# Channel attention and a look-up-table FFN: Wo loaded early, x groups issued from ScalarE, look-up results built in the low parts' place

## The reference

```python
x = x + attn(layernorm(x), Wq, Wk, Wv, Wo)
x = x + ffn(layernorm(x), lut, gate_idx, up_idx, down_idx)

def attn(x, Wq, Wk, Wv, Wo):           # attention over channels, not over tokens
    qT, kT, vT = (swapaxes(x @ w, 1, 2) for w in (Wq, Wk, Wv))
    weights = softmax(einsum('bes,bfs->bef', qT, kT) / 4)      # 512 x 512 a batch
    return swapaxes(einsum('bef,bfs->bes', weights, vT), 1, 2) @ Wo

def ffn(x, lut, gate_idx, up_idx, down_idx):
    gate, up = x @ lut[gate_idx].T, x @ lut[up_idx].T
    return (silu(gate) * up) @ lut[down_idx].T
```

## Time and profile before

| | |
|---|---|
| median of 3 runs | 1040.51 us (1039.37 to 1041.04) |
| the profiled execution | 1041.32 us; its span 1039.2 us, mean granted clock 0.993 |
| TensorE busy | 1000.8 us, 96% of the span |
| VectorE, ScalarE, GpSimd busy | 485.5, 449.5, 140.4 us |
| VectorE busy from 240 to 360 us | 118.69 of 120 us |

### The profile page before, as it was taken

How to read it: one execution, slowest core, us unless ns; L and a number is a source line. 1 busy time by engine, 2 the same in 40 slices (tenths; PEclk the granted TensorE clock), 3 DMA queues, 4 the chain that set the end, 5 groups by cost and what they waited for, 6 DMA issues and landing times.

```text
span 1039.2 us, 12623 instructions
## 1 busy us (share of the span) xinstructions
PE 1000.8 (96%) x4612; PEld 825.3 (79%) x4612; DVE 485.5 (47%) x1019; ACT 449.5 (43%) x720; POOL 140.4 (14%) x149
## 2 busy tenths in 40 slices
PE   5999889999989999999999999999999999999998
PEld 4988768787777778888888888888888888888886
DVE  5899899899999942312131213111311131112001
ACT  4898798879998821121222122212221222122111
POOL 2332300000000000111111011101110111011111
PEclk9999989999999999999999999999999999999999
DMA  8899902300112182200220002002200020001001
GB/s 258 201 162 147 175 20 86 130 21 34 51 49 72 63 307 98 82 1 1 81 81 1 1 1 82 1 1 81 81 1 1 1 81 1 1 1 41 1 1 40
DMA packets 45050, 65.89 MB, mean 63 GB/s; under 512 B 22128, under 2 KB 32256, under 8 KB 40448
## 3 DMA queue, kind: packets, MB, share of 16 engines
q1 hardware_dynamic: 31808, 56.70, 16.5%
q0 software_dynamic: 8864, 6.43, 5.5%
q10 hardware_dynamic: 4320, 1.97, 0.7%
HBM read 44.05 MB, written 25.10 MB: 67 GB/s over the span
## 4 chain that ended last, share of the span: by engine, by line
PE 83%; DVE 9%; issue 3%; ACT 2%; POOL 1%; DMA 1%; POOLq 0%; SPq 0%; ACTq 0%; DVEq 0%
PE bank L1014 41%; PE bank L1022 21%; PE bank L956 14%; PE bank L1038 4%; DVE part L1181 2%; DVE bn L1158 1%; PE bank L970 1%; PE bank L1003 1%; DVE picked L1181 1%; POOL rstd L726 1%; ACT part L764 1%; DMA xg<-in_L_attn_x 1%; DVE xg_lo L1200 1%; DVE part L1225 1%; DVE bit_mask L1188 0%
## 5 line engine op out<-in xcount | busy, mean ns | idle before, releaser
L1014 PE MATMUL bank<-x2t_hi,w_hi 128*128 128x512 f32 (+1 forms) x704 | 276.3, 392 | 10.8 <-DVE w_lo L1200 7.1
L1014 PE MATMUL bank<-x2t_lo,w_hi 128*128 128x512 f32 (+1 forms) x704 | 275.3, 391 | 0.0
L1014 PE MATMUL bank<-x2t_hi,w_lo 128*128 128x512 f32 (+1 forms) x704 | 275.2, 391 | 0.0
L1405 DVE TENSOR_TENSOR h_full<-bank,h_gate 128x512 f32<-128x512 f32 (+1 forms) x66 | 45.6, 691 | 396.0 <-PE bank L1014 396.0
L1014 PEld LDWEIGHTS bank<-x2t_hi,w_hi 128*128 128x128 f32 (+1 forms) x704 | 130.9, 186 | 42.7 <-DVE w_lo L1200 9.0
L764 ACT ACTIVATE part<-high_bit,lut,lut_step 128x512 f32<-128x512 uint8 x198 | 154.0, 811 | 16.1 <-DVE part L1181 11.0
L1014 PEld LDWEIGHTS bank<-x2t_lo,w_hi 128*128 128x128 f32 (+1 forms) x704 | 131.2, 186 | 29.8
L1014 PEld LDWEIGHTS bank<-x2t_hi,w_lo 128*128 128x128 f32 (+1 forms) x704 | 131.2, 186 | 29.2
L721 POOL TENSOR_TENSOR h_lo<-h_full,h_hi 128x512 fp32r<-128x512 f32 (+1 forms) x66 | 85.3, 1292 | 507.4 <-ACT h_hi L932 507.4
L929 ACT ACTIVATE h_gate<-bank 128x512 f32<-128x512 f32 (+1 forms) x66 | 39.5, 598 | 256.4 <-PE bank L1014 256.4
L1022 PE MATMUL bank<-w_hi,h_hi 128*128 128x512 f32 (+1 forms) x324 | 129.8, 401 | 0.1
(11 more groups left out here) (145 smaller groups left out, 1291.9 us busy)
## 6 DMA issues: line engine op xcount, KB each, us to landing
xg<-in_L_attn_x SPq DMA_DIRECT2D x7, 1024.0 KB, 6.4
x1a<-in_L_attn_x SPq DMA_DIRECT2D x4, 1024.0 KB, 4.8
out_dram<-x1a SPq DMA_DIRECT2D x4, 1024.0 KB, 4.2
x1b<-in_L_attn_x SPq DMA_DIRECT2D x3, 1024.0 KB, 4.9
m_hi<-m_scratch SPq DMA_DIRECT2D x3, 1024.0 KB, 4.8
m_lo<-m_scratch SPq DMA_DIRECT2D x3, 1024.0 KB, 8.2
out_dram<-x1b SPq DMA_DIRECT2D x3, 1024.0 KB, 3.9
h_scratch<-h_kept_hi SPq DMA_DIRECT2D x10, 256.0 KB, 2.0
```

The lines of the kernel that those rows point to most:

```text
L1014: last = pe.matmul(tile[0:n, :], a, x, start=(k == 0 and j == 0), stop=(k == K - 1 and j == 2))
L1405: dve.tensor_tensor(h_full[0:n, :], bank[5][0:n, :], h_gate[0:n, :], ALU.mult).then_inc(h_done, 1)
```

## The change

1. **Wo** gets four tiles `raw_o` of its own (where `x1a` will lie later), which SP loads one after the other after the last piece of Wq. The load of the first x block into `x1` waits for the last split of Wo.
2. **x groups** 3 to 7 are issued by ScalarE: group 3 after the second normalised tile, group g + 3 after the first normalised tile of group g.
3. **Index transfers** stand at other items; the turns of units 0 to 2 are at 6 to 8 rather than 9 to 11, and early stores go to an item that is a multiple of 4.
4. **Head of the Gram stage**: two statistics of group 1 before `gram_low` 1, two after; `gram_low` 2 ahead of `stats_shift` 2. Where a group begins, `gram_in` stands before `gram_n`.
5. **The look-up's result** is built where `w_lo` of the unit will lie; `low` then works in place. The two `picked` tiles are gone, the other leaves have seven tiles: those for j = 2 and 3 are doubled, so that they wait for merges of unit u - 2 and not u - 1. The waits for space that stood ahead of `w_hi` in five units (12, 15, 21, 27, 30) stand ahead of leaf 0.
6. **New tables** `ACT_LOOKS` and `DVE_LOOKS`.

The diff, cut to its core (tile addresses, helpers' signatures and most of the tables are left out):

```diff
@@
         all_tiles = at("all_tiles", 0, [P, 101, D], F32)
...
+        W_PLACE, Y_PLACE, PART_PLACE, Z_PLACE = 94, 95, 97, 99
+        def place_of(u, j):
+            one, five = PART_PLACE + u % 2, PART_PLACE + 1 - u % 2
+            y, z = Y_PLACE + u % 2, Z_PLACE + u % 2
+            return {0: (w_at[u // 3] + 6) // 2 + u % 3, 1: one, 2: y, 3: z, 4: W_PLACE, 5: five, 6: one, 7: z}[j]
...
-            if u and j in (1, 2, 3, 5):
-                eng.wait_ge(merged, merge_count(u - 1, {1: M_45, 2: M_RY, 3: M_67, 5: M_WX}[j]))
+            if u and j in (1, 5):
+                eng.wait_ge(merged, merge_count(u - 1, {1: M_45, 5: M_WX}[j]))
+            if u >= 2 and j in (2, 3):
+                eng.wait_ge(merged, merge_count(u - 2, {2: M_RY, 3: M_67}[j]))
...
-            if j == 0 and u >= 2:
-                eng.wait_ge(w_lo_done, u - 1)
+            if j == 0 and u == 12:
+                eng.wait_ge(product_done, K * (number[(MIX, 0)] + 1))
...
-        narrow_at = [2, 10, 16, 24, 30, 34]
-        turn_at = [9, 10, 11, 16, 18, 20, 22, 24, 26, 28, 29, 30] + list(range(31, 52))
-        store_at = [place + 2 for place in turn_at]
+        narrow_at = [2, 10, 18, 28, 32, 36]
+        turn_at = [6, 7, 8, 14, 15, 16, 22, 24, 26, 27, 28, 29, 32, 33, 34, 35, 36, 37] + list(range(38, 53))
+        store_at = [-(-(place + 2) // 4) * 4 if place < 28 else place + 2 for place in turn_at]
...
+            if i == 0:
+                timeline += [("stats_of", (1, t)) for t in range(2)]
             if i + 1 < T * NG:
                 timeline.append(("gram_low", i + 1))
             if i == 0:
-                timeline += [("stats_of", (1, t)) for t in range(T)]
+                timeline += [("stats_of", (1, t)) for t in range(2, T)]
                 settle(2)
+            if i == 1:
                 timeline.append(("stats_shift", 2))
...
-                if g >= 4:
-                    sp.wait_ge(xg_normed, T * (g - 3))
-                sp.dma_start(xg[g % 4][:], xb_dram[g]).then_inc(xg_loaded[g % 4], 16)
...
                     if arg == (WQ, K - 1):
+                        for k in range(K):
+                            sp.dma_start(raw_o[k][:], wo_in[k * P:(k + 1) * P, :]).then_inc(raw_o_loaded[k], 16)
                         sp.wait_ge(xg_normed, T * 7)
...
-                act.copy(w_hi[c][:, kind, :], picked[u % 2][:]).then_inc(w_hi_done, 1)
+                act.copy(w_hi[c][:, kind, :], tile_of(u, 0)).then_inc(w_hi_done, 1)
...
+                    if i == 1:
+                        load_gram(3)
+                    if t == 0 and 1 <= g and g + 3 < NG:
+                        load_gram(g + 3)
...
                 if stage == "raw":
                     w, k = arg
                     r = K * w + k
-                    act.wait_ge(raw_loaded[r % 2], 16 * (r // 2 + 1))
                     if w == WO:
+                        act.wait_ge(raw_o_loaded[k], 16)
                         act.wait_ge(product_done, K * (number[(PROD, 1)] + 1))
...
-                low(w_lo[c][:, kind, :], picked[u % 2][:], w_hi[c][:, kind, :]).then_inc(w_lo_done, 1)
+                low(w_lo[c][:, kind, :], tile_of(u, 0), w_hi[c][:, kind, :]).then_inc(w_lo_done, 1)
```

More of the change, by code:

```diff
@@ L99, in preln_attention_ghost_ffn @@
         raw_v = [at(f"raw_v{k}", 156 + 2 * k, [P, D], F32) for k in range(K)]
+        raw_o = [at(f"raw_o{k}", 48 + 2 * k, [P, D], F32) for k in range(K)]
         raw = [at(f"raw{i}", 184 + 2 * i, [P, D], F32) for i in range(2)]
@@ L171, in preln_attention_ghost_ffn @@
         raw_loaded = [sem(f"raw_loaded{i}") for i in range(2)]
+        raw_o_loaded = [sem(f"raw_o_loaded{k}") for k in range(K)]
         raw_v_loaded = [sem(f"raw_v_loaded{k}") for k in range(K)]
@@ L287, in make_leaf @@
                 eng.wait_ge(merged, merge_count(u, {6: M_01, 7: M_23}[j]))
-            if j == 0 and u >= 2:
-                eng.wait_ge(w_lo_done, u - 1)
-            return tile_of(u, j)[:], high_bit[u % 2][:], lut_step[:, j:j + 1], lut[:, j:j + 1]
+            if j == 0 and u == 12:
+                eng.wait_ge(product_done, K * (number[(MIX, 0)] + 1))
+            if j == 0 and u == 15:
+                eng.wait_ge(product_done, K * (number[(FOLD, 0)] + 1))
+            if j == 0 and u == 21:
+                eng.wait_ge(m_stored, 16 * 2 * B)
+            if j == 0 and u == 27:
+                eng.wait_ge(x2_turned, 2 * K)
+            if j == 0 and u == 30:
+                eng.wait_ge(second_stored, 16)
+            return tile_of(u, j), high_bit[u % 2][:], lut_step[:, j:j + 1], lut[:, j:j + 1]
         timeline = []
@@ L335, in preln_attention_ghost_ffn @@
                     settle(g + 2)
-            if i + AHEAD + 1 < T * NG:
-                timeline.append(("gram_n", i + AHEAD + 1))
-            if i + AHEAD < T * NG:
-                timeline.append(("gram_in", i + AHEAD))
+            steps = [(name, i + ahead) for name, ahead in (("gram_n", AHEAD + 1), ("gram_in", AHEAD)) if i + ahead < T * NG]
+            timeline += steps if (i + AHEAD + 1) % T else steps[::-1]
             index_steps(i)
@@ L594, in _ @@
                     turn_idx(arg)
-                if stage == "gram" and arg % T == 2 and 4 <= arg // T + 4 < NG:
-                    load_gram(arg // T + 4)
                 if stage == "raw":
                     after = K * arg[0] + arg[1] + 1
-                    if after < K * WV:
+                    if after < K * WO:
                         load_raw(after // K, after % K)
                     if arg == (WQ, K - 1):
+                        for k in range(K):
+                            sp.dma_start(raw_o[k][:], wo_in[k * P:(k + 1) * P, :]).then_inc(raw_o_loaded[k], 16)
                         sp.wait_ge(xg_normed, T * 7)
@@ L757, in fetch_idx, with load_gram @@
                 act.dma_start(idx_in[u % 3][:], idx_dram[u]).then_inc(idx_back[u % 3], 16)
+            def load_gram(g):
+                if g >= 4:
+                    act.wait_ge(xg_normed, T * (g - 3))
+                act.dma_start(xg[g % 4][:], xb_dram[g]).then_inc(xg_loaded[g % 4], 16)
             def make_leaves(u, some):
@@ L1177, in stats_shift, with merge @@
                                          op1=ALU.mult).then_inc(done, 1)
-            def merge(bit, keep, other):
-                return dve.copy_predicated(keep[:], bit_mask[bit][:], other[:])
+            def merge(u, bit, keep, other):
+                return dve.copy_predicated(tile_of(u, keep), bit_mask[bit][:], tile_of(u, other))
             def pairs_of(byte):
@@ L1215, in look_up @@
                 for u in range(U):
[L1216 removed]
                     dve.wait_ge(bits_found, 3 * u + 1)
                     dve.wait_ge(leaf_made, leaf_count(u, 0))
[L1219 removed]
+                    merge(u, 0, 0, 1).then_inc(merged, 1)
                     yield
                     dve.wait_ge(leaf_made, leaf_count(u, 2))
[L1222 removed]
+                    merge(u, 0, 2, 3).then_inc(merged, 1)
                     yield
@@ L1243, in look_up @@
                     dve.wait_ge(leaf_made, leaf_count(u, 7))
-                    merge(0, one, z).then_inc(merged, 1)
+                    merge(u, 0, 6, 7).then_inc(merged, 1)
                     yield
```

67 lines of the change are left out of this document (29 added, 38 removed).

## The result

The changed kernel takes 1036.45 us (median of 9 runs, 1034.69 to 1037.34) against 1040.65 (9 runs) for the one before; the ratio is 0.9954, interval 0.9943 to 0.9965, so 3.6 to 5.9 us less. It is faster, but by about half of the 9.5 us forecast (4.8 by the ratio, 4.2 by the medians): inside the whole range, above the likeliest case's own 1028 to 1034. The profiled execution took 1034.96 with a span of 1032.9, 6.3 less than the span before. It is one of the faster ones.

The account below looks back on a forecast made before the run. VectorE's idle time until unit 31's low part was taken as the bound: 2.3 + 4.1 + 2.5 + 2.0 - 1.1 = 9.8, less 0.6 at the tail, plus 0.3 in block 1, gave 9.5 off, 1031.0 us; range 1026.5 to 1037.5.

Parts of the forecast that it names:

- likeliest case: The main forecast for the whole kernel's time, with its own range of 1028 to 1034 us; chance 0.58.
- Wo early: Near 113 us, early Wo loads remove ScalarE's and VectorE's waits for its first piece, saving VectorE 4.1 us idle.
- the sum's end: At chunk 10's up product in block 0, TensorE waits 2.0 us for the low part, so it starts at 351.0.
- The head: At the Gram stage's start, reordered statistics and low parts make VectorE and tile 2 2.3 us earlier.
- Leaf waits: In the look-up, doubled tiles for leaves 2 and 3 save 2.5 of VectorE's 4.2 us waiting for leaves.
- the 2 us given as a sign: Sign for the seven tiles in the look-up: merges' waits for leaves would be under 2 us.
- Other waits: From 20 to 240 us, VectorE's other waits for TensorE shrink by 2.0 us, between 0 and 5.
- Item 16: At Gram item 16, nine look-up steps make TensorE pause 4.0 us, then lower clock; 1.1 us of VectorE waiting.
- slower case: Rival: look-up runs ahead at the products' cost; TensorE pays 4.4 at item 16; 1046.7 us, chance 0.09.
- The tail's + 0.6: At the look-up's end, unit 31's low part stands behind `h_low` of block 1, chunk 9, costing 0.6 us.
- Edits costed at nothing: Result in place, leaves' target tile, moved waits, x groups from ScalarE and the x1 load's wait: set at no cost.
- small gain: Rival: waits for leaves and banks stay, VectorE only meets them later; 4.7 us gain, 1035.8 us, chance 0.18.

Follow-up runs that it names:

- b_same: The kernel before, unaltered, run again for a second trace; median 1040.7 us, ratio 0.9992.
- b_wo: The kernel before with only the early loading of Wo into four tiles of its own added; median 1040.2 us, ratio 0.9996.
- b_head: The kernel before with only the new order at the head of the Gram stage and at group starts; median 1037.7 us, ratio 0.9972.
- a_oldtable: The changed kernel with the look-up tables of the kernel before; median 1036.8 us, ratio 0.9963.
- a_same: The changed kernel, unaltered, run again for a second trace; median 1036.6 us, ratio 0.9966.
- a_same2: The changed kernel, unaltered, once more as a measure for kernels beside it on the same chip; median 1036.8 us, ratio 0.9976.
- a_headold: The changed kernel with the old order at the head of the Gram stage and at group starts; median 1043.7 us, ratio 1.0018.
- a_woraw: The changed kernel with Wo loaded through the two old raw tiles again; median 1039.8 us, ratio 0.9978.
- o_five: The changed kernel with the tables of before and five part tiles, leaves 2 and 3 in one tile each; median 1037.9 us, ratio 0.9968.
- a_tail: The changed kernel with unit 31's low part moved behind the first merge of unit 32; median 1033.6 us, ratio 0.9934.
- a_xsp: The changed kernel with x groups 3 to 7 issued by SP again; median 1036.4 us, ratio 0.9963.
- a_narrow: a_tail with the narrowing copies of the indices at their old items; look-up steps also moved unintentionally; median 1038.6 us, ratio 0.9973.
- a_idxold: a_tail with narrowing, transposes and stores of the indices at their old items; look-up steps also moved unintentionally; median 1051.4 us, ratio 1.0095.
- a_tail2: a_tail run again beside the unaltered changed kernel; median 1033.4 us, ratio 0.9921.
- a_fill: a_tail with spare TensorE matmuls ahead of the first MIX product and batch 0's first FOLD product; median 1033.2 us, ratio 0.9934.

## Why the prediction was wrong, step by step

**The bound was right.** VectorE's idle time up to unit 31's low part, taken off that part's start, leaves nearly the same time in every trace:

| trace | idle before it | its start | start less idle |
|---|---|---|---|
| before | 32.4 | 360.15 | 327.8 |
| b_same | 32.6 | 360.65 | 328.0 |
| b_wo | 30.9 | 358.80 | 327.9 |
| b_head | 29.1 | 356.51 | 327.4 |
| a_oldtable | 29.2 | 356.40 | 327.2 |
| changed | 25.3 | 352.09 | 326.8 |
| a_same | 27.0 | 354.14 | 327.1 |
| a_same2 | 26.4 | 353.36 | 327.0 |
| a_headold | 34.3 | 361.30 | 327.0 |
| a_woraw | 32.4 | 359.05 | 326.7 |

So VectorE's work ahead of this part hardly changes, and what counts is its idle time in all. That does not say that two savings add up, and they did not. The forecast saved 9.8; the three traces of the changed kernel save 5.6 to 7.3 against b_same.

**The step that failed is the term "Wo early", 4.1.** It was read from one execution, and taken off the end whole. In b_same and b_head VectorE has no wait for Wo; b_wo, which removes it for certain, gains 0.4 us (interval -0.7 to 1.6). In SP's queue the second piece of Wo, behind transposes that wait for index stores to land, goes out here in the first trace of the kernel before, and then in b_same:

```profile
112.11 0.58 SPq L576 DMA_DIRECT2D raw<-in_L_attn_Wo  x1
```

```profile
107.89 0.58 SPq L576 DMA_DIRECT2D raw<-in_L_attn_Wo  x1
```

Even in the first, shorter waits followed: from 80 to 130 us VectorE is idle 4.2 us more than in b_same (5.8 and 1.5), from 130 to 280 us 3.0 less (9.2 and 12.2). That the other engines caught up in the meantime is the likely reason; no run tests it. It holds for the kernel before alone: in the changed one, VectorE in a_woraw's trace idles 4.8 us more from 80 to 130 us than in the changed kernel's first (8.8 and 4.0; 2.0 of it is the late index), and no less behind (9.3 against 7.1 to 8.9).

**The second step is the sum's end.** The working found that TensorE would wait 2.0 us for chunk 10's up product, and put the clock behind this pause at nothing, though it expected the lower clock behind the pause at item 16. The pause itself costs nothing more, since the low part sets the start either way: from its start to the end of the span it is 679.0 to 679.3 us with a pause of 0 (before, b_same, o_five) and with one of 1.45 to 1.48 (b_wo, b_head, a_oldtable). With 2.57 it is 680.8 (1032.9 less 352.09): 1.8 lost. The clock fell there in all six traces that have this pause (680.6 to 680.9). a_tail shows that mending the place brings 3 to 6 us. With nothing for Wo and 1.8 less at the end the forecast's 9.5 becomes 3.6; measured are 4.2 to 4.8.

**The other terms.** The head, 2.3: 2.9 alone, the one large gain and most of the result. Leaf waits, 2.5: 4.9 in the first trace of the kernel before (the sum took only the 4.2 for `part`, without `picked`), 6.5 in b_same, 3.1 now, so 1.8 or 3.4, and not under the 2 us given as a sign. The seven tiles alone are not what did it, as o_five shows under the old tables; it came with the new tables, or with both together. Other waits, 2.0: from 130 to 280 us VectorE idles 7.1, 8.9 and 8.6 us in the three traces, 3.3 to 5.1 less than in b_same, but from 80 to 130 it idles 4.0 rather than 1.5, as `wa_lo` and `smax` now wait 1.9 and 1.4. Item 16: TensorE's pause was 2.97 rather than 4.0, and the clock behind it fell in a_same but not in the first trace; VectorE's wait 0.8 rather than 1.1. (The working's own numbers give 51.7 there, not 51.5, and its slower case has 4.4 for the same pause.) The tail's + 0.6: one more low part does stand ahead, but VectorE's work up to there came out 0.7 to 1.2 us shorter (the table's last column); why is open. Edits costed at nothing: x groups on ScalarE cost nothing (a_xsp); the result in place and the moved waits cost nothing that a_oldtable shows beside b_head.

**What was not in the forecast at all** is late indices of unit 5. With the new tables unit 5's indices are loaded near 87 us, 10 us ahead of their need. In 6 of the 11 traces with new tables (a_narrow and a_idxold left aside) the longest landing was over 12 us, and VectorE waited 1.6 to 6.4; in none of the 7 with the old tables did it wait. From issue to landing (min, median, max, 60 to 130 us) in b_same, the changed kernel and a_tail2, from the view of the tile `idx_in`:

```profile
DMA to landing us min/median/max: 1.9/4.6/10.3
```

```profile
DMA to landing us min/median/max: 2.0/4.1/7.5
```

```profile
DMA to landing us min/median/max: 2.2/4.6/15.8
```

Two traces of the same program up to there differ like this: the load of 87.3 or 87.4 us lands after 7.3 us in the changed kernel's first trace and after 17.1 in a_tail. The wait is made good only in part: from 80 to 130 us VectorE is idle 8.9 us in a_tail and 3.9 in a_fill, and unit 31's low part starts at 354.69 and 351.62. The three traces of the changed kernel itself have no such wait, so what it costs the median isn't known. Whether part 3 or the earlier need brings this is open; in a_narrow and a_idxold, where the load goes out only at 92 us, it landed within 8 us.

Of the rivals, the small gain came true by its time (1035.8), but not by its reason: it kept the Wo term whole, and the leaf waits did shrink. That the measured time lies inside the whole range is partly luck, as neither the sum nor this rival reckoned with a Wo term of nothing. The slower case has nothing to show for it. The rule of the Trainium skill that the prediction weighed for the index stores (page "SBUF — State Buffer", section "Who interferes with whom": a two-port instruction of VectorE can block GpSimd) left no mark here: two of GpSimd's issues took 1.14 us together at 37.19 us, as before, and unit 1's indices had landed by 42.9, 4.0 us before VectorE read them at 46.9.

## What to carry to other kernels

A wait behind a DMA may belong to the execution and not to the kernel: take a second trace before it goes into a sum, and ask what stood in the queue ahead of it. Where one engine's stream bounds a stretch, its idle time up to the last thing that others need is the right quantity, but a wait taken out at one place may come back at the next. Check also what happens where the stream hands over: here one low part, made five short instructions sooner, was worth 3 to 6 us, and without it the new tables showed nothing in the time. Reordering the head of the Gram stage gave 2.9 of the 4.8 us at no cost.
